# Weight pass of a four-layer graph network: 42 of 50 columns in bf16 parts split by VectorE, weighing on ScalarE, one buffer for each group

## What is computed

```python
def _L2_gnn_ref(x, edge_weight, W, b, edge_src, edge_dst):
    msgs = x[edge_src] * edge_weight[:, None]
    agg = jax.ops.segment_sum(msgs, edge_dst, num_segments=x.shape[0])
    return agg @ W.T + b
...
h = jnp.maximum(_layernorm(x, axis=-1), 0.0)
x = x + _L2_gnn_ref(h, edge_weight, L2_gnn_W, L2_gnn_b, src, dst)
```

## Time and profile before

| | |
|---|---|
| median of 3 runs | 4967.69 us (4963.65 to 4969.53) |
| the profiled execution's own time | 4966.04 us |
| its span, first to last instruction | 4964.2 us |
| granted TensorE clock, mean | 0.965 of full |
| the weight pass in it | 2552.81 to 3232.46 us |
| busy share of the span | PE 90%, DVE 83%, ACT 58%, POOL 16% |

### The profile page before, as it was taken

The page is one execution under the profiler, slowest core; times in us unless marked ns, Lnnn a source line. Parts: engine busy times, 40 slices in busy tenths (PEclk is TensorE's granted clock), DMA queues, the critical chain, the costliest instruction groups (busy, mean ns, idle before and its releaser), DMA issues.

```text
span 4964.2 us, 254617 instructions
## 1 busy us (share of the span) xinstructions
PE 4459.2 (90%) x101536; PEld 4017.0 (81%) x101536; DVE 4111.3 (83%) x6842; ACT 2873.8 (58%) x9065; POOL 801.3 (16%) x1001
## 2 busy tenths in 40 slices
PE   1999999669999999499969999969999998999998
PEld 1677777469999999488869999958888886888887
DVE  7799999889999999888888989977767776767676
ACT  1999999512222222477743333356666665666665
POOL 2455555311111111000012222200000000000000
PEclk7999999879999999799979999989999999999999
DMA  1000000068887887000024444433333333333333
GB/s 53 2 1 2 2 1 2 17 191 254 255 253 252 255 254 231 14 0 0 0 64 121 121 119 121 117 82 98 99 96 98 98 96 92 101 98 100 99 99 83
DMA packets 305222, 501.40 MB, mean 101 GB/s; under 512 B 76918, under 2 KB 78454, under 8 KB 305126
## 3 DMA queue, kind: packets, MB, share of 16 engines
q1 hardware_dynamic: 303782, 499.39, 34.6%
q0 software_dynamic: 576, 0.52, 0.1%
q10 hardware_dynamic: 768, 0.16, 0.0%
HBM read 408.40 MB, written 91.57 MB: 101 GB/s over the span
## 4 chain that ended last, share of the span: by engine, by line
PE 51%; issue 17%; DVE 15%; ACT 12%; POOL 3%; DMA 1%; DVEq 1%; ACTq 0%; POOLq 0%; SPq 0%
PE PS L1514 19%; ACT arena L863 11%; PE PS L1507 9%; PE PS L1311 7%; PE PS L1289 5%; PE PS L1291 5%; DVE arena L1823 4%; DVE arena L2467 3%; POOL arena L792 2%; PE PS L1306 2%; PE PS L1545 1%; PE PS L1443 1%; PE PS L1428 1%; PE PS L1318 1%; DVE arena L2393 1%
## 5 line engine op out<-in xcount | busy, mean ns | idle before, releaser
L1823 DVE TENSOR_TENSOR arena<-iotab,arena 128x1024 bf16<-128x1024 bf16 (+3 forms) x1887 | 1749.2, 960 | 228.1 <-PE PS L1514 167.7
L1040 ACT ACTIVATE arena<-PS 128x384 bf16<-128x384 f32 x2450 | 1001.4, 498 | 543.2 <-PE PS L1507 543.2
L1514 PE MATMUL PS<-arena 32*128 32x193 bf16 (+1 forms) x41552 | 994.8, 242 | 44.6 <-DVEq L2468 41.1
L1514 PEld LDWEIGHTS PS<-arena 32*128 32x128 bf16 x41552 | 838.3, 92 | 149.5 <-DVEq L2468 58.0
L863 ACT ACTIVATE arena<-PS,m 128x196 bf16<-128x196 f32 x1813 | 739.7, 448 | 21.7 <-PE PS L1148 21.7
L1507 PE MATMUL PS<-Hp,arena 128*128 128x192 bf16 (+1 forms) x4900 | 536.5, 248 | 35.8 <-DVE Hp L1667 35.4
L1289 PE MATMUL PS<-Hp,arena 128*128 128x72 bf16 x7350 | 500.0, 198 | 43.9 <-DVE arena L2169 40.3
L1020 ACT ACTIVATE arena<-PS,ewB 128x64 f32<-128x64 f32 x1176 | 257.4, 330 | 420.6 <-PE PS L1351 420.6
L1291 PE MATMUL PS<-arena 128*128 128x72 bf16 x7350 | 500.6, 198 | 0.0
L1507 PEld LDWEIGHTS PS<-Hp,arena 128*128 128x128 bf16 x4900 | 382.1, 99 | 145.9 <-issue 84.9
L1155 PE MATMUL PS<-arena,tmp 128*128 128x262 bf16 x1813 | 450.8, 277 | 17.0 <-DVE tmp L1823 14.8
(11 more groups left out here) (376 smaller groups left out, 7954.6 us busy)
## 6 DMA issues: line engine op xcount, KB each, us to landing
arena<-hots SPq DMA_DIRECT2D x735, 256.0 KB, 2.6
arena<-codes SPq DMA_DIRECT2D x245, 512.0 KB, 5.1
hots<-arena SPq DMA_DIRECT2D x245, 256.0 KB, 5.2
arena<-hots SPq DMA_DIRECT2D x147, 320.0 KB
arena<-codes SPq DMA_DIRECT2D x49, 640.0 KB, 5.6
hots<-arena SPq DMA_DIRECT2D x49, 320.0 KB, 5.5
rows_h<-Hn SPq DMA_DIRECT2D x4, 1568.0 KB, 9.8
rows_l<-Y SPq DMA_DIRECT2D x1, 1764.0 KB, 9.8
```

The costliest lines, as they stand in the source:

```text
L1040: act.activation(RG[ROW_BUFFER[g]][:, 2 * i:2 * i + 2, 0:RW], ps[PAIR_BANK[q]][:, 0:2 * RW].rearrange("p (k c) -> p k c", k=2), ACT.Copy). ...
L1514: last = pe.matmul(ps[2 + q][:, b * SW:b * SW + SW - o], one_hot[32 * q:32 * q + 32, b * P:(b + 1) * P], rows_of[32 * q:32 * q + 32, 0:SW ...
L1823: return dve.tensor_tensor(to.rearrange("p k (n t) -> p k n t", t=4), iota_of[:, 0:n].rearrange("p (n t) -> p n t", t=4)[:, None, :, :] .t ...
```

## The change

All six groups now take one way. ACT weighs all 50 columns (`weigh_rows`, 50 instructions a window where there were 24) into one buffer for each group (`W3q`, `w_OB`, six of each where there were three and three). For groups 0 to 4 (42 columns) DVE makes both subtractions (`rest` and `lowest_part`) and PE scatters three bf16 parts; group 5 (8 columns) stays f32. POOL does nothing in the pass but the few. The gathers run three groups ahead of the scatters in three pairs of PSUM banks (`bank_at`), as in the attention pass. The codes are laid out in `w_cdw` by ACT, in two halves (`own_codes`; half 0 for groups 0 to 2, half 1 for groups 3 to 5), and half 1 of the next window is written only when `f_ohd` says that all six one-hot matrices of this window are made. `evict` no longer waits for itself, and the sums stand in two banks instead of three.

```diff
-        w_OD = [cv.take(GS[0] * P).rearrange("p (k n) -> p k n", n=P) for _ in range(3)]
-        w_OB = [cv.take(GS[1] * P, bf16).rearrange("p (k n) -> p k n", n=P) for _ in range(3)]
...
+        w_OB = [cv.take(n * P, bf16).rearrange("p (k n) -> p k n", n=P) for n in GS[0:NG - 1]] + \
+            [cv.take(GS[NG - 1] * P).rearrange("p (k n) -> p k n", n=P)]
...
-                    for i in range(3):
-                        g = 2 * i + 1
-                        act.wait_ge(f_gath, d * NG + (2 * NN + g + 4))
-                        act.wait_ge(b_scat, d * 3 + (i + 1))
...
+                def own_codes(dx, h):
+
+                    if not is_zero(dx):
+                        act.wait_ge(f_ohd, dx * NG + (2 * NN - 3 + 3 * h))
+                    cols = slice(0, HALF) if h == 0 else slice(HALF, CPW)
+                    act.activation(w_cdw[:, cols, :], cdA3[:, bass.ds(dx, 1), cols].rearrange("p w c -> p (w c)")
+                                   [:, :, None].to_broadcast((P, cols.stop - cols.start, 4)), ACT.Copy).then_inc(f_codes, 1)
+
+                def weigh_rows(dx, last):
+                    for g in range(NG):
+                        act.wait_ge(f_gath, dx * NG + (2 * NN + g + 4))
+                        if not is_zero(dx):
+                            act.wait_ge(b_scat, dx * NG + (g + 1 - NG))
                         for k in range(GS[g]):
...
+                        done.then_inc(b_whole, 1)
+                        if g >= 4 and not last:
+                            own_codes(dx + 1, g - 4)
...
+            def weight_pass():
+                def one_hots(dx, g):
+
+                    if g % 3 == 0:
+                        dve.wait_ge(f_codes, dx * 2 + (2 * WINDOWS + g // 3 + 1))
+                    if not is_zero(dx):
+                        dve.wait_ge(b_scat, dx * NG + (g + 1 - NG))
+                    compare(w_OB[g], iotab1, w_cdw[:, G0[g]:G0[g] + GS[g], :]).then_inc(f_ohd, 1)
...
+                def operands(dx, g):
+                    if g < NG - 1:
+                        rest(dx, g)
+                    one_hots(dx, g)
+                    if g < NG - 1:
+                        lowest_part(dx, g)
...
+                    for g in range(NG):
+                        if not (last and g + 1 == NG):
+                            operands(dx + (g + 1) // NG, (g + 1) % NG)
+                        if g == 1 and not first:
                             evict(dx - 1, 1)
-                        if i == 0:
+                        if g == 2:
                             few(dx)
-                        if i == 2:
+                        if g == 4:
                             evict(dx, 0)
```

More of the change, by code:

```diff
@@ L427, in gnn_stack @@
             "f_mx", "f_exp", "f_scat", "f_sum", "f_accout", "f_ohm", "f_step"))
[L428 to L429 removed]
+        b_whole, b_rest, b_low, b_scat = (sem(n) for n in (
+            "b_whole", "b_rest", "b_low", "b_scat"))
         f_mg, f_mstep, f_mmx, f_mexp, f_misc, f_codes = (sem(n) for n in (
@@ L448, in bank_at, with wait_weighed @@
             m = GS[g] // 2
-            a = 2 * (g % 2) + (k >= m)
-            return ps[a][:, (k % m) * WIDE:(k % m) * WIDE + WIDE]
+            a = ((0, 1), (2, 3), (5, 7))[g % 3][k // m]
+            return ps[a][:, (k % m) * DIM:(k % m + 1) * DIM]
+        def wait_weighed(engine, dx, g):
+            engine.wait_ge(b_whole, dx * NG + (g + 1))
         def gathered_half(g, h):
@@ L1012, in _ @@
             with act.If(runs < 2):
[L1013 to L1022 removed]
+                def own_codes(dx, h):
[9 more added lines that the diff above has]
+                            act.wait_ge(b_scat, dx * NG + (g + 1 - NG))
+                        for k in range(GS[g]):
+                            done = act.activation(W3q[g][:, k, 0, :], bank_at(g, k), ACT.Copy,
+                                                  scale=ewB[:, bass.ds(dx * CPW + (G0[g] + k), 1)])
+                        done.then_inc(b_whole, 1)
+                        if g >= 4 and not last:
+                            own_codes(dx + 1, g - 4)
+                own_codes(0, 0)
+                own_codes(0, 1)
+                weigh_rows(0, False)
+                with act.Fori(1, LASTW) as d:
+                    weigh_rows(d, False)
+                weigh_rows(LASTW, True)
             parts_of_h(4)
@@ L1334, in attend_edges, with gather_rows_at @@
                 body(LASTW, True)
-            def gather_rows_at(dx, i, whole):
-                g = 2 * i + (not whole)
+            def gather_rows_at(dx, g):
                 pe.wait_ge(f_hot[g], dx * 16 + 16)
[L1340 to L1343, removed]
+                if g >= 3:
+                    wait_weighed(pe, dx, g - 3)
+                elif not is_zero(dx):
+                    wait_weighed(pe, dx - 1, g + 3)
                 for k in range(GS[g]):
@@ L1350, in gather_rows_at, with scatter_parts @@
                             rhs = Hp[:, bass.ds(dx, 1), a * DIM:(a + 1) * DIM].rearrange("p w c -> p (w c)")
-                        last = pe.matmul(bank_at(g, k)[:, 0:DIM], w_OT[g % 3][:, k * P:(k + 1) * P], rhs,
+                        last = pe.matmul(bank_at(g, k), w_OT[g % 3][:, k * P:(k + 1) * P], rhs,
                                          start=(a == 0), stop=(a == PARTS - 1))
                 last.then_inc(f_gath, 1)
-            def scatter_whole(dx, i):
-                g = 2 * i
-                h = i // 2
+            def scatter_parts(dx, g):
+                h = g // 3
                 to = ps[4 + 2 * h][:, 0:DIM]
-                pe.wait_ge(f_whole, dx * 3 + (2 * NN + i + 3))
+                if g < NG - 1:
+                    pe.wait_ge(b_low, dx * (NG - 1) + (g + 1))
+                else:
+                    wait_weighed(pe, dx, g)
                 pe.wait_ge(f_ohd, dx * NG + (2 * NN + g + 1))
-                if i != 1:
+                if g % 3 == 0:
                     pe.wait_ge(f_accout, dx * 2 + (2 * 2 * WINDOWS + h + 1))
                 for k in range(GS[g]):
-                    last = pe.matmul(to, w_OD[i][:, k, :], Wq[i][:, k, :], start=(i != 1 and k == 0),
-                                     stop=(i == 1 and k == GS[g] - 1))
-                last.then_inc(f_scat, 1)
-                if i == 2:
+                    if g == NG - 1:
+                        last = pe.matmul(to, w_OB[g][:, k, :], W3q[g][:, k, 0, :], start=False, stop=False)
+                        continue
+                    for a in range(PARTS):
+                        last = pe.matmul(to, w_OB[g][:, k, :], Wup[g][:, k, a, :],
+                                         start=(g % 3 == 0 and k == 0 and a == 0),
+                                         stop=(g == 2 and k == GS[g] - 1 and a == PARTS - 1))
+                last.then_inc(b_scat, 1)
+                if g == NG - 1:
                     pe.wait_ge(f_misc, 3)
@@ L1373, in scatter_whole, with body @@
                     last.then_inc(f_sum, 1)
[L1375 to L1379, removed]
-                if i == 0:
[L1381 to L1387, removed]
-            def weigh_edges():
[L1390 to L1411, removed]
+            def weigh_edges():
+                def body(dx, last):
+                    for g in range(NG):
+                        if g < NG - 3:
+                            gather_rows_at(dx, g + 3)
+                        elif not last:
+                            gather_rows_at(dx + 1, g + 3 - NG)
+                        scatter_parts(dx, g)
+                for g in range(3):
+                    gather_rows_at(0, g)
+                with pe.Fori(0, LASTW) as d:
+                    body(d, False)
+                body(LASTW, True)
             pe.wait_ge(s_begin, 1)
@@ L2316, in body @@
                 def body(dx, first, last):
[L2317 to L2323, removed]
-                            weigh(*to_come)
-                        rest(dx, i)
-                        if i == 0 and not first:
+                    for g in range(NG):
+                        if not (last and g + 1 == NG):
+                            operands(dx + (g + 1) // NG, (g + 1) % NG)
+                        if g == 1 and not first:
                             evict(dx - 1, 1)
-                        if i == 0:
+                        if g == 2:
                             few(dx)
-                        if i == 2:
+                        if g == 4:
                             evict(dx, 0)
-                dve.sem_inc(b_out, 1)
-                at[0], at[1] = ofs, 0
-                one_hots(0, 0, True)
-                weigh(0, 0)
+                operands(0, 0)
                 body(0, True, False)
                 with dve.Fori(1, LASTW) as d:
-                    at[0], at[1] = d * 4 + (ofs - 1), 0
                     body(d, False, False)
-                at[0], at[1] = ofs + 4 * LASTW - 1, 0
                 body(LASTW, False, True)
                 evict(LASTW, 1)
-                evict_parts(LASTW)
```

(3 more changed lines are left out.)

62 lines of the change are left out of this document (16 added, 46 removed).

## The result

The changed kernel takes 4988.2 us, median of 5 runs (4987.48 to 4994.14), against 4963.9 us for the kernel before in the same comparison: a ratio of 1.0049, interval 1.0037 to 1.0061. It is slower by half a per cent, and it was forecast at 4985. The profiled execution took 4987.48 us, its span is 4985.2 us.

The account below looks back on a forecast made before the run. A DVE-ACT loop was taken as the bound: 11.21 + 0.13 + 0.60 + 2.16 + 0.03 = 14.13 us a window against 13.61; with edges the pass ends 17.5 us later, giving 4985 us, range 4958 to 5014.

Parts of the forecast that it names:

- PE is freed and that is not seen: PE's window work falls to 10.9 us, 2.4 us less, but PE waits in short pieces and shows no saving.
- The circle bounds: DVE's sixth one-hot matrix, ACT's next codes layout and weighings, then DVE's next subtraction lie in series: 14.13 us a window.
- DVE 11.21: DVE's way from its start on group 0 to the end of group 5's one-hot matrix: 11.21 us a window.
- hand over to ACT: From the end of DVE's sixth one-hot matrix to ACT's start on the codes: 0.13 us, including a register wait.
- codes and jump: On ACT, from the start of the codes' layout through jump and register instructions to the first weighing: 0.60 us.
- weighings and hand over: ACT's ten weighings of the next group 0, 2.16 us, then 0.03 us until DVE starts.
- no change: Rival: jump and registers run ahead, ACT's part 0.4 us shorter, loop near 13.7 us, 4965 us; 16 in 100.
- Weighing at 0.206 us: ACT's pace per weighing instruction in the pass, from a profile row; fifty a window take 10.3 us.
- Edges: Start and end of the weight pass: window 1 at about 2571.7, window 48 at 3235.8, pass ending 3250.0, 17.5 us later.
- The clock rival: PE's clock falls to half in the pass because PE idles: 21.8 us a window, 5350 us; 4 in 100.
- The faster rival: The loop does not bind and DVE's work does: some 11.5 us a window, 4860 us; 6 in 100.
- PE's work: PE's matmuls in a window after the change, gathers, bf16 and f32 scatters and the few: 10.9 us.

Follow-up runs that it names:

- the run with the circle closed: Changed kernel with the second subtraction of groups 0 to 4 back on GpSimd, the codes' layout left where it was: 5057.26 us, ratio 1.0174.
- With the circle open: Changed kernel with the layout of the codes' second half moved behind group 1's weighing in the next window: 4861.73 us, ratio 0.9782.

## Why the prediction was right

- **PE is freed and that is not seen.** Right. PE idles 102 us of 600, and 1.4 us of matmuls a window more cost nothing.
- **The circle bounds.** Right, and shown both ways: moving the layout out of it gives 2.7%, moving 0.47 us of DVE's work out of it gives 22 us.
- **Its size.** 14.13 us were forecast, 14.14 measured. The parts: DVE 11.21 (11.26), hand over to ACT 0.13 (0.12), codes and jump 0.60 (0.57), weighings and hand over 2.19 (2.19). The jump's price was the least certain, read off one pass of the same loop's jump in the kernel before, with an estimate on top for the register instructions; with a term 0.4 us shorter the forecast would have been "no change".
- **Weighing at 0.206 us.** Right: 34 in 7.06 us with the last alone at 0.31 are 0.205 us. The estimate of 240 ns from start to start, worked out from the Trainium skill's figures (ScalarE: Activation LUTs, What ACT_TABLE_LOAD costs), is not what this instruction does here.
- **The number.** Near, in part by luck. The forecast started from 4967.69 us for the kernel before, which took 4963.9 in this comparison. So the slowdown is 24.3 us where 17.3 were forecast (4985 less 4967.69), and of the 7.0 us that are missing only 3.2 show in 4988.2 against 4985.
- **Edges.** A little off. Window 1 begins at 2569.80 and window 48 at 3233.92, 664.1 us as forecast, but the pass began 3.1 us earlier than in the trace before, and at its end the last f32 group and the few ran at half clock:

```profile
3233.92 0.82 DVE L2269 TENSOR_TENSOR arena<-arena 128x640 f32<-128x640 f32 x1 [2.41 <-ACT arena L1022]
...
3245.32 3.65 PE L1378 MATMUL PS<-arena 128*128 128x64 f32 x16
...
3250.74 0.56 DVE L2409 TENSOR_SCALAR inv<-agg 128x392 f32<-128x392 f32 x1 [0.24 <-DVE agg L2291]
```

  3.65 us for what takes 1.98 in other windows of this trace; the granted clock from 3245 to 3250 us is 0.50. The pass from PE's first gather to this last line is 700.1 us (from 2550.62), before 678.8 (from 2553.70 to 3232.46): 21.3 us more, 17.5 were forecast. The 3.8 us too few are 1.2 at the start (window 1 begins 19.2 us after PE's first gather, 18.0 were reckoned) and 2.6 at the end (16.8 us from window 48 on, 14.2 were reckoned). The earlier begin of the pass hides 3.1 of them; why it began earlier is not known. PE waited for hots twice, 3.47 and 1.49 us, both in the first window.
- **The clock rival.** It was not the bound, but it was not absent either: see below. The sign "PE at full clock with about 78% busy" failed; it is 83% at 0.97 of the clock.
- **The faster rival's numbers.** I gave 11.5 us a window and 4860 us for a pass in which the loop does not bind; the run with the layout moved has 11.30 and 4861.73 (by its ratio, 4856 where the kernel before takes 4963.9).
- **PE's work.** A term of the sum of PE's work was mis-sized, 10.9 us for 10.6: I took a bf16 scatter matmul at 32 ns from one pair of starts; in the changed kernel 24 of them take 0.73 us from start to start (2862.82 to 2863.55), 30 ns each. It was on no bound.

## What to carry to other kernels

Add up each engine's work, and then walk the program order for a circle: an instruction of engine A that waits for B's last one of this round and stands ahead of A's first one of the next, which B needs. Its time is the sum of both ways, however idle all engines look; the sign is two waits, each once a round, that release each other. A small instruction that recycles a buffer belongs where its wait is long met, a group or two later, and not at the end of the round.

Work that goes back from GpSimd to VectorE can be nearly free, and work that goes the other way can cost more than it saves. Here each of the five subtractions on GpSimd, 1.42 to 1.77 us long, cost the VectorE instruction that met it 0.7 to 0.9 us in the run with the circle closed; price each meeting at up to what is left of GpSimd's instruction when VectorE's would start (at 2856.59 1.04 us were left, and 0.90 were lost).

## What the runs showed of the hardware that was not expected

PE's clock fell to half in short pieces in the steady pass of the changed kernel, although its longest wait there was 1.6 us. The windows view of three neighbouring stretches:

```profile
2841.40:2855.30 13.90, 11.19 (x296) 10.67 (x293) 11.15 (x19) 10.55 (x53) 0.00 (x0) 1.00 0.41 113
2855.40:2858.80 3.40, 3.40 (x70) 3.40 (x67) 3.40 (x8) 2.68 (x14) 0.00 (x0) 0.50 0.16 63
2858.80:2869.00 10.20, 8.79 (x229) 8.55 (x226) 7.45 (x13) 7.68 (x39) 0.00 (x0) 1.00 0.50 132
```

Full clock (2.4 GHz), half (1.2 GHz), full; over the whole steady pass 0.97 of full. The piece begins behind PE's wait of 1.63 us for the subtraction of group 0. But 46 windows have this wait of 1.63 us, and only 12 hold such a piece. PE's timeline behind the same wait, one window earlier and in this one:

```profile
2840.95 1.07 PE L1381 MATMUL PS<-arena 128*128 128x64 bf16 x30 [1.63 <-DVE arena L2274]
...
2855.09 1.58 PE L1381 MATMUL PS<-arena 128*128 128x64 bf16 x30 [1.63 <-DVE arena L2274]
```

What tips it is not shown. 24 gathers took 1.47 us in the piece where they take 0.86, and no window took longer: the distance between windows is 14.14 us with such a piece and without. ACT was held up by PE, but its wait for the sixth matrix took that in: 2.23 us at the end of this window, 3.07 at the end of the one before. I had argued that short waits with matmuls between them would keep the full clock; they did not quite. With the circle open (longest wait of PE and its weight loads 0.6 us) the clock is 1.00 from 2600 to 3050 us.
